# Experts' tiles in a new order, and the results of two groups of tokens fetched and normalised before the last scatters

## The chip, the cores and the metric

One core of a Trainium2 chip runs the whole kernel. The metric is the time of the device for one execution, in microseconds (us), as a median over runs. A TensorE (PE), a VectorE (DVE), a ScalarE (ACT), a GpSimd (POOL) and the queue of SyncE (SP) work beside each other and wait for each other by semaphores.

## The reference

The input x is 128 sequences of 64 tokens with 128 features, so 8192 tokens. Four layers are added to x one after the other, each behind a layer norm:

```
x = x + tanh(g_xattn[0]) * attention_16_heads(layernorm(x), ctx, ctx)        # heads of 8
x = x + tanh(g_ffn[0])   * experts(layernorm(x))                             # 8 experts, 2 per token, gelu, hidden 512
x = x + tanh(g_xattn[1]) * attention_1_head(layernorm(x), ctx, mask)         # tanh on the values
x = x + tanh(g_ffn[1])   * quantised_ffn(layernorm(x))                       # x and h rounded to 8 bits by their extremes
# experts: probs = softmax(x @ router.T); the two largest, divided by their sum, weigh
#          gelu(x @ w_fc[e] + b_fc[e]) @ w_proj[e] + b_proj[e]
```

## The kernel before, in words

Tokens stand 128 to a tile, four tiles make a group (QUAD, in the code also "super"), so there are 64 tiles in 16 groups; two groups are a chunk of 1024 tokens. The residual x stays in on-chip memory (`x_sb`) for the whole kernel. There are three programs (STAGES), with all engines meeting between them.

**First program, first attention and routing.** `layer0_and_experts` computes the first attention group by group. Beside it, VectorE picks two experts for every token, and POOL sends each token's normalised row twice by indirect DMA (L553) to `tokens_to`, a buffer in device memory with one region per expert. Rows come in the order of the tokens, so the first 1024 tokens lie in the first 1024 rows of their experts' regions at most.

**Experts.** The rows of an expert are cut into tiles of 512 rows (RT), some into half tiles of 256. There are ETILES = 40 places for them: EARLY = 13, whose numbers are known after five of eight chunks, and 27 late ones, nine times two full tiles and a half. Two tables say for each place at which row it begins and whose weights it takes. `early_tables` makes them in the first attention, in chained small operations of VectorE; `late_ends`, `tiles_and_halves`, `rows_and_jumps` and `half_tables` make the late ones piece by piece between the experts' tiles 4 to 7. In both, all tiles of expert 0 come first, then those of expert 1, and so on. SP loads a tile's rows (L350) and weights (L358, L368) in the order of the places; PE multiplies, ScalarE and VectorE take the sums, and POOL scatters the results by indirect DMA (L572), four instructions for a full tile, two for a half, to `results`, where each token has two rows. `returned` counts landed scatters in a ring of eight tiles (YRING).

**The seam.** When all scatters are back, SP loads `results` of groups 0, 1, 2 and 3 to 4 (`load_two`, L1838) and the rows of a mask (L430). At the same time VectorE, PE and ScalarE quantise the last layer's weights (L1754 to L1769, L846 to L854), and ScalarE sends them to device memory (`w_out`). VectorE adds the two result rows of group 0 (`first_sums`) and takes its statistics; ScalarE normalises it. VectorE adds group 1. POOL's last work are constants for the next program (`terms`). The mask load waits for `w_out`.

**Second attention.** In `layer1_attention` each engine has a program of steps s = 0 to 17, one per group, written out in order. POOL adds the results of groups 2 and up (`add_results`, L1948 and L1950) and normalises groups 3 and up (`normalise`, L1956 and L1959). VectorE takes statistics (`rows_of`, L2102 and L2105), reciprocals of the deviations by BATCHES of groups (`factors`, L2110), maxima of the scores (L2121), and the weighted sums of two steps earlier (L2130 to L2136). ScalarE takes square roots by batch (`roots`, L1980), normalises groups 1 and 2 (L2000), evicts products and takes exponentials (L2024). In POOL's stream the order is:

```
        for n in range(SUMS_IN_FRONT, 7):
            add_results(n)
        for n in (3, 4):
            normalise(n)
            add_results(n + 4)
        for n in range(5, SUPERS):
            if n + 4 < SUPERS:
                add_results(n + 4)
            normalise(n)
```

A normalising waits for the reciprocals of its whole batch (`rstd_ready`), and statistics for POOL's addition (`pool_added`). The third program, `layer1_ffn`, is not touched.

## Time and profile before

| what | us |
|---|---|
| three runs | 921.99, 925.02, 928.18 (median 925.02) |
| the profiled execution | 912.86 |
| its span, first to last instruction | 911.0 |
| VectorE busy | 715.8 |
| PE busy | 711.5 |
| POOL busy | 578.8 |
| ScalarE busy | 570.3 |
| first expert's product to last scatter | 374.4 to 690 |
| second attention | 702.2 to 791.8 |

The shares of busy time are means over stages with different limits. All times of rows are those of the profiled execution, counted from its first instruction, and its own time is 12 us under the median of the runs.

### The profile page before, as it was taken

To read this page: it belongs to the slowest core of one execution; us is meant where nothing else is said; L and a number is where in the kernel's file an instruction comes from. 1 tells how busy PE (TensorE), PEld (TensorE's weight loads), DVE (VectorE), ACT (ScalarE), POOL (GpSimd) and SP (SyncE) were. 2 spreads that over 40 slices of the span, in tenths; PEclk is the share of its full clock that TensorE was granted. 3 is DMA by queue.
4 is the path that set the end of the run, shared out by engine and by line. 5 is a ranking of instruction groups with operands and counts; after the bars stand their busy time and mean duration, and the time that the engine had idled before them with its cause. 6 is when DMAs were issued, how large, how long until landed. Compare 5 with 4: busy or idle time off the path is not lost. (4 is left out here: it accounts for less than half of the span.)

```text
span 911.0 us, 19681 instructions
## 1 busy us (share of the span) xinstructions
PE 711.5 (78%) x6547; PEld 556.5 (61%) x6550; DVE 715.8 (79%) x1835; ACT 570.3 (63%) x1176; POOL 578.8 (64%) x565
## 2 busy tenths in 40 slices
PE   5888799999999998689088899897972788556535
PEld 3666677777777776567066687776761566322224
DVE  4999999888888988477075677777763699889988
ACT  4556466767666664565165566766653888578745
POOL 4575487788887777646755545564555996088820
PEclk9999899999999989899588999999995899876569
DMA  8413632413232223657267778887835933000005
GB/s 244 122 37 127 102 106 86 140 61 130 89 107 84 83 98 115 232 162 216 64 192 226 243 223 276 247 253 217 251 124 175 350 107 107 24 1 0 1 23 163
DMA packets 95428, 127.69 MB, mean 140 GB/s; under 512 B 20528, under 2 KB 65152, under 8 KB 94304
## 3 DMA queue, kind: packets, MB, share of 16 engines
q1 hardware_dynamic: 85760, 108.00, 39.0%
q0 software_dynamic: 8672, 17.99, 5.7%
q8 instruction: 54, 0.88, 0.4%
q10 hardware_dynamic: 896, 0.43, 0.2%
q14 instruction: 46, 0.38, 0.1%
HBM read 82.76 MB, written 43.53 MB: 139 GB/s over the span
## 5 line engine op out<-in xcount | busy, mean ns | idle before, releaser
L572 POOL DMA_INDIRECT m_results<-a_probs,e_to x142 | 144.2, 1015 | 110.2 <-ACT a_probs L805 65.4
L783 ACT ACTIVATE room<-a_ps_s,e_bias 128x512 f32<-128x512 f32 (+1 forms) x160 | 102.2, 651 | 101.2 <-PE a_ps_s L1089 48.9
L581 POOL TENSOR_TENSOR a_probs<-a_probs,a_top 128x1024 f32<-128x1024 f32 x64 | 122.0, 1907 | 66.6 <-DVE a_top L1633 65.2
L553 POOL DMA_INDIRECT m_tokens_to<-r_rows,r_place x128 | 129.7, 1013 | 34.3 <-issue 32.0
L1662 DVE CAST e_hp<-room 128x512 fp32r<-128x512 f32 (+1 forms) x160 | 67.2, 420 | 88.4 <-remote 39.7
L700 ACT ACTIVATE a_probs_t<-a_ps_pt 128x512 f32<-128x512 f32 x128 | 70.2, 592 | 84.0 <-PE a_ps_pt L989 82.8
L1664 DVE TENSOR_TENSOR e_hp<-room,e_hp 128x512 fp32r<-128x512 f32 (+1 forms) x160 | 103.2, 645 | 5.6
L973 PEld LDWEIGHTS a_ps_o<-a_vals,a_probs_t 128*64 128x64 f32 x2048 | 71.2, 144 | 30.6 <-issue 29.8
L1594 DVE TENSOR_TENSOR a_probs<-a_ps_s,a_mask 128x1024 f32<-128x1024 f32 x64 | 78.0, 1219 | 15.0 <-PE a_ps_s L870 8.3
L973 PE MATMUL a_ps_o<-a_vals,a_probs_t 128*64 128x18 f32 x2048 | 79.1, 217 | 8.4 <-issue 6.6
L1633 DVE TENSOR_REDUCE a_top<-a_probs 128x16 f32<-128x1024 f32 x64 | 77.2, 1206 | 0.1
L989 PE MATMUL a_ps_pt<-ident,a_probs 128*128 128x128 f32 x512 | 74.3, 293 | 2.0 <-DVE n_values L1412 1.5
L2430 DVE TENSOR_REDUCE d_hpeak<-d_hid 128x1 f32<-128x2048 f32 (+1 forms) x36 | 70.7, 2044 | 3.6 <-ACT d_hid L2329 3.6
L989 PEld LDWEIGHTS a_ps_pt<-ident,a_probs 128*128 128x128 f32 x512 | 64.4, 152 | 3.5 <-DVE n_values L1412 2.7
L1099 PE MATMUL a_ps_pt<-e_hp,e_weights 128*128 128x512 f32 (+1 forms) x100 | 40.0, 400 | 31.9 <-issue 31.9
L1085 PE MATMUL a_ps_s<-e_xt,e_weights 128*128 128x512 f32 (+1 forms) x160 | 64.9, 405 | 0.0
L1089 PE MATMUL a_ps_s<-e_xt,e_weights 128*128 128x512 f32 (+1 forms) x160 | 60.8, 380 | 3.1 <-DVE e_xt L1671 3.1
L1086 PE MATMUL a_ps_s<-e_xt,e_weights 128*128 128x512 f32 (+1 forms) x160 | 60.6, 379 | 0.0
L2329 ACT ACTIVATE d_hid<-d_ps_h,d_b,d_outscale 128x512 f32<-128x512 f32 x64 | 46.2, 779 | 8.7 <-PE d_ps_h L2369 7.1
L634 ACT ACTIVATE room<-a_ps,a_own_bk,a_own 128x512 f32<-128x512 f32 x64 | 44.7, 787 | 2.5 <-PE a_ps L890 2.5
L1117 PE MATMUL a_ps_pt<-ident,room 128*128 128x128 f32 x142 | 24.7, 294 | 22.2 <-ACT room L797 16.5
L805 ACT ACTIVATE a_probs<-a_ps_pt,room 128x128 f32<-128x128 f32 x142 | 40.8, 373 | 1.8 <-PE a_ps_pt L1117 1.0
(396 smaller groups left out, 1908.3 us busy)
## 6 DMA issues: line engine op xcount, KB each, us to landing
e_weights<-m_weights_to SPq DMA_DIRECT2D x80, 512.0 KB
m_weights_to<-r_parts SPq DMA_DIRECT2D x8, 1024.0 KB
room<-m_tokens_to SPq DMA_DIRECT2D x31, 264.0 KB
c_two<-m_results SPq DMA_DIRECT2D x3, 1536.0 KB, 11.8
a_ctx_in<-in_ctx_dram SPq DMA_DIRECT2D x17, 256.0 KB, 3.0
m_keys_t<-n_keys SPq DMA_DIRECT2D x16, 256.0 KB
m_values<-n_values SPq DMA_DIRECT2D x16, 256.0 KB
out_dram<-x_all SPq DMA_DIRECT2D x15, 256.0 KB, 2.3
```

The source lines that it names most:

```text
L553: pool.indirect_dma_start(tokens_to, bass.IndirectOffsetOnAxis(ap=place[:, k, q:q + 1], axis=0), rows[:, c % RING, q % CT, k, :], None).th ...
L572: pool.indirect_dma_start(results, bass.IndirectOffsetOnAxis(ap=to[:, v, r:r + 1], axis=0), y[:, v, r], None).then_inc(returned[v], 16)
L581: pool.tensor_tensor(probs[:, j], probs[:, j], top[:, j].unsqueeze(2).broadcast_to([P, HEADS, SEQ]), ALU.subtract).then_inc(shifted, 1)
L700: act.activation(probs_t[:, j % 2, 4 * h:4 * h + 4, :], ps_pt[h][:], ACT.Exp).then_inc(pt_sb, 1)
L783: act.activation(h[:, c, at], ps_h[c][:, at], ACT.Gelu_apprx_tanh, bias=bias[:, n % ROWS, c:c + 1]).then_inc(h_sb, 1)
L973: mm = pe.matmul(ps_o[SEQ * b:SEQ * b + SEQ, cols], probs_t[:, (j + 1) % 2, gr, SEQ * b:SEQ * b + SEQ], vals[(t - 3) // QUAD % 2][:, (j + ...
L989: mm = pe.transpose(ps_pt[h][:, k, :], probs[:, (t + 2) % 4, 8 * h + 2 * k:8 * h + 2 * k + 2] .rearrange("p j k -> p (j k)"), ident[:])
L1594: dve.tensor_tensor(probs[:, j].rearrange("p (i k) q -> p i k q", i=BANDS), ps_s[:, :, j % 2], mask[:].unsqueeze(1).unsqueeze(1).broadcast ...
L1633: dve.tensor_reduce(top[:, j], probs[:, j], AX_X, ALU.max).then_inc(top_ready, 1)
L1662: dve.tensor_copy(hp[:, c, 0, at], h[:, c, at]).then_inc(h_hi, 1)
L1664: dve.tensor_tensor(hp[:, c, 1, at], h[:, c, at], hp[:, c, 0, at].bitcast(F32), ALU.subtract).then_inc(h_lo, 1)
L2430: dve.tensor_reduce(hpeak[:, e, column:column + 1], h, AX_X, op).then_inc(hpeak_ready, 1)
```

## The change

The tables put tiles in two classes: first at most two full tiles of every expert (with the odd halves of experts that have fewer), then all others. So each table operation works on 16 classes (CLASSES) instead of 8 experts, on one partition. Whatever belongs to the first 1024 tokens is then at the latest in place FIRST_CHUNK_END - 1 = 33 of 40.

Behind its last weight load SP waits for the scatters up to place 33, then loads the results of groups 0 and 1 into an own buffer (`early_two`, in `pad`). VectorE adds them between its steps on the last layer's weights, takes statistics of eight tiles, and ScalarE normalises both groups. POOL's constants are made after tile 13's scatters. The loads for groups 2 to 4 stay where they were.

In the second attention VectorE adds group 2 itself. Step 0 no longer waits for normalisings of groups 1 and 2: ScalarE takes the root and normalises group 2 after the exponentials of group 0, and the root of groups 3 and 4 at the end of its step 0. POOL adds three groups in front instead of five, and stays three groups ahead of its normalising instead of four.

```diff
+CLASSES = 2 * EXPERTS
+FIRST_TWO = 2 * QUAD
+FIRST_CHUNK_END = EARLY + 3 * (EXPERTS - 1)
...
+    early_two = pad[:].rearrange("p e r w -> p (e r w)")[:, 0:4 * ST].rearrange("p (s t k c) -> p s t k c", s=2, t=QUAD, k=2)
...
-    f_rows, f_mv = stats[:, 0:QUAD], mv[:, 0:QUAD]
-    f_std, f_rstd, f_nmr = (n[:, 0:QUAD] for n in (rstd2, rstd, nmr2))
+    f_rows, f_mv = stats[:, 0:FIRST_TWO], mv[:, 0:FIRST_TWO]
+    f_std, f_rstd, f_nmr = (n[:, 0:FIRST_TWO] for n in (rstd2, rstd, nmr2))
...
+        for n in range(FIRST_CHUNK_END - YRING, FIRST_CHUNK_END):
+            sp.wait_ge(returned[n % YRING], rows_returned(n))
+        for n in range(2):
+            load_two(sp, g, n, early_two[:, n:n + 1])
...
-        for n in range(EARLY_LOADS):
+        for n in range(2, EARLY_LOADS):
             load_two(sp, g, n, two[:, TWO_LOADS[n][0]:TWO_LOADS[n][1]])
...
         for n in range(1, ETILES):
             return_results(n)
-        pool.memset(magic[:, 0:1], MAGIC).then_inc(terms, 1)
-        pool.memset(magic[:, 1:2], -MAGIC).then_inc(terms, 1)
...
-        pool.wait_ge(terms, 12)
+            if n == EARLY:
+                pool.memset(magic[:, 0:1], MAGIC).then_inc(terms, 1)
+                pool.memset(magic[:, 1:2], -MAGIC).then_inc(terms, 1)
+                pool.memset(eps[:], LN_EPS).then_inc(terms, 1)
...
+                pool.wait_ge(terms, 12)
...
-        act.wait_ge(f_mv_ready, QUAD)
+        act.wait_ge(f_mv_ready, FIRST_TWO)
         act.activation(f_std[:], f_mv[:, :, 1], ACT.Sqrt, bias=power[:, 0, 0:1]).then_inc(f_std_ready, 1)
...
-        for k in range(QUAD):
-            act.activation(xn[:, 0, k], x_sb[:, k], ACT.Identity, scale=f_rstd[:, k:k + 1], bias=f_nmr[:, k:k + 1])\
+        for k in range(FIRST_TWO):
+            act.activation(xn[:, k // QUAD, k % QUAD], x_sb[:, k], ACT.Identity, scale=f_rstd[:, k:k + 1], bias=f_nmr[:, k:k + 1])\
                 .then_inc(f_xn_ready, 1)
...
-            then(dve.tensor_reduce(experts, passed, AX_X, ALU.add))
-            then(dve.tensor_reduce(rows_at, jumps, AX_X, ALU.add))
+        def beside_classes(x, n):
+            return x[:, 1:].unsqueeze(1).broadcast_to([1, n, CLASSES])
+
+        def early_look_up():
...
+            then(dve.tensor_tensor(early_jump[:], early_past[:], skip.unsqueeze(1).broadcast_to([1, EARLY, CLASSES]), ALU.mult))
+            then(dve.tensor_reduce(experts, early_past[:], AX_X, ALU.add))
+            then(dve.tensor_reduce(rows_at, early_jump[:], AX_X, ALU.add))
             then(dve.scalar_tensor_tensor(out=rows_at, in0=numbers, scalar=float(RT), in1=rows_at,
                                           op0=ALU.mult, op1=ALU.add))
-            then(dve.tensor_scalar(experts, experts, EXPERTS - 1.0, None, ALU.min))
+            then(dve.tensor_scalar(least, experts, float(EXPERTS), -float(EXPERTS), ALU.is_ge, ALU.mult))
+            then(dve.tensor_tensor(experts, experts, least, ALU.add))
...
+                then(dve.memset(one16, 1.0))
+                then(dve.memset(tile_end, 0.0))
+                then(dve.memset(odd_end, 0.0))
+                then(dve.memset(row_at, float(EXPERTS * REGION)))
+                then(dve.memset(odd_at, float(EXPERTS * REGION)))
+                then(dve.tensor_tensor(count, total[0:1, :, 0], base[0:1], ALU.subtract))
+                then(dve.tensor_scalar(ntile, count, 1.0 / RT, -0.5 + 0.5 / RT, ALU.mult, ALU.add))
+                then(dve.tensor_scalar(ntile, ntile, MAGIC, MAGIC, ALU.add, ALU.subtract))
+                then(dve.tensor_scalar(vt[:, 0:EXPERTS], ntile, 2.0, None, ALU.min))
+                then(dve.tensor_tensor(vt[:, EXPERTS:], ntile, vt[:, 0:EXPERTS], ALU.subtract))
+                then(dve.tensor_scalar(skip, vt, -float(RT), float(REGION), ALU.mult, ALU.add))
+                last = skip[:, EXPERTS - 1:EXPERTS]
+                then(dve.tensor_scalar(last, last, float(2 * RT - EXPERTS * REGION), None, ALU.add))
             if nth == 1:
-                tile_ends()
-                look_up(EARLY)
+                then(dve.tensor_tensor_scan(tile_end[:, 1:], one16, vt, 0.0, ALU.mult, ALU.add))
+                early_look_up()
...
+                then(dve.tensor_scalar(capped, tile_end, float(EARLY), None, ALU.min))
+                then(dve.tensor_tensor(used16, capped[:, 1:], capped[:, 0:CLASSES], ALU.subtract))
+                then(dve.tensor_tensor(used, used16[:, 0:EXPERTS], used16[:, EXPERTS:], ALU.add))
...
+                beside(dve.tensor_tensor(vt[:, EXPERTS:], ntile, vt[:, 0:EXPERTS], ALU.subtract))
+                beside(dve.scalar_tensor_tensor(out=row_at[:, EXPERTS:CLASSES], in0=vt[:, 0:EXPERTS], scalar=float(RT),
+                                                in1=row_at[:, 0:EXPERTS], op0=ALU.mult, op1=ALU.add))
+                beside(dve.scalar_tensor_tensor(out=oddv[:, 0:EXPERTS], in0=gone, scalar=2.0, in1=odd[:],
+                                                op0=ALU.is_lt, op1=ALU.mult))
+                for n in range(2):
+                    beside(dve.scalar_tensor_tensor(out=odd_at[:, EXPERTS * n:EXPERTS * n + EXPERTS], in0=gone,
+                                                    scalar=float(RT), in1=base[0:1], op0=ALU.mult, op1=ALU.add))
+            if turn == 3:
+                beside(dve.tensor_tensor_scan(tile_end[:, 1:], one16, vt, 0.0, ALU.mult, ALU.add))
+                beside(dve.tensor_tensor(oddv[:, EXPERTS:], odd[:], oddv[:, 0:EXPERTS], ALU.subtract))
+                beside(dve.tensor_tensor(odd_jump, odd_at[:, 1:], odd_at[:, 0:CLASSES], ALU.subtract))
+                beside(dve.tensor_tensor(skip, row_at[:, 1:], row_at[:, 0:CLASSES], ALU.subtract))
...
-            if t == 7 and turn < 2:
+            if t == 7 and turn < 3:
...
 
+        def first_sums(n):
+            four = slice(n * QUAD, n * QUAD + QUAD)
+            dve.wait_ge(two_in[n], 16)
+            dve.tensor_tensor(early_two[:, n, :, 0], early_two[:, n, :, 0], early_two[:, n, :, 1], ALU.add).then_inc(f_summed, 1)
+            dve.wait_ge(f_summed, n + 1)
+            dve.tensor_tensor(x_sb[:, four], x_sb[:, four], early_two[:, n, :, 0], ALU.add).then_inc(f_added, 1)
+
         dve.memset(w_magic[:, 0:1], MAGIC).then_inc(w_dve, 1)
         dve.memset(w_magic[:, 1:2], -MAGIC).then_inc(w_dve, 1)
         dve.wait_ge(w_in2, 32)
         for n in range(2):
             dve.tensor_reduce(w_peak[:, n:n + 1], w[:, n].rearrange("p a b -> p (a b)"), AX_X, ALU.max,
                               apply_absolute_value=True).then_inc(w_dve, 1)
+        first_sums(0)
         dve.wait_ge(w_pe, 1)
         dve.tensor_reduce(w_both, ps_h[2][0:2, 0:P], AX_X, ALU.max).then_inc(w_dve, 1)
         dve.wait_ge(w_pe, 2)
         dve.tensor_scalar(wscale[:], ps_h[3][:, 0:2], 1.0 / 127.0, 1e-8, ALU.mult, ALU.max).then_inc(w_dve, 1)
         dve.wait_ge(w_dve, 6)
         dve.reciprocal(w_inv[:], wscale[:]).then_inc(w_dve, 1)
+        first_sums(1)
         for n in range(2):
             dve.wait_ge(w_act, n + 1)
             dve.tensor_scalar(w[:, n], w[:, n], MAGIC - 127.0, MAGIC + 127.0, ALU.max, ALU.min).then_inc(w_dve, 1)
 
-        def first_sums(n):
-            four = slice(n * QUAD, n * QUAD + QUAD)
-            dve.wait_ge(two_in[n], 16)
-            dve.tensor_tensor(two[:, n, :, 0], two[:, n, :, 0], two[:, n, :, 1], ALU.add).then_inc(f_summed, 1)
-            dve.wait_ge(f_summed, n + 1)
-            dve.tensor_tensor(x_sb[:, four], x_sb[:, four], two[:, n, :, 0], ALU.add).then_inc(f_added, 1)
-
-        first_sums(0)
-        dve.wait_ge(f_added, 1)
...
-        for k in range(QUAD):
+        dve.wait_ge(f_added, 2)
+        for k in range(FIRST_TWO):
             dve.bn_stats(f_rows[:, k], x_sb[:, k]).then_inc(f_stats, 1)
-        for k in range(QUAD):
+        for k in range(FIRST_TWO):
...
-        first_sums(1)
...
-BATCHES = ((0, 1), (1, 2), (2, 3), (3, 5), (5, 8), (8, 12), (12, 16))
+BATCHES = ((0, 2), (2, 3), (3, 5), (5, 8), (8, 12), (12, 16))
...
-SUMS_IN_FRONT = 2
+SUMS_IN_FRONT = 3
...
+        for n in range(SUMS_IN_FRONT, 6):
             add_results(n)
         for n in (3, 4):
             normalise(n)
-            add_results(n + 4)
+            add_results(n + 3)
         for n in range(5, SUPERS):
-            if n + 4 < SUPERS:
-                add_results(n + 4)
+            if n + 3 < SUPERS:
+                add_results(n + 3)
             normalise(n)
 
...
         def roots(n):
             of = slice(BATCHES[n][0] * QUAD, BATCHES[n][1] * QUAD)
-            act.wait_ge(mv_ready, (BATCHES[n][1] - 1) * QUAD)
+            act.wait_ge(mv_ready, (BATCHES[n][1] - 2) * QUAD)
...
         evict_x(0)
-        roots(1)
-        normalise(1)
         act.wait_ge(ahead_in, 96)
         evict_q(0)
         evict_x(1)
-        roots(2)
-        normalise(2)
-        roots(3)
         for s in range(SUPERS + 1):
...
+            if s == 0:
+                roots(1)
+                normalise(2)
             if s + 2 < SUPERS:
                 evict_x(s + 2)
-            if s in (1, 5, 8):
-                roots({1: 4, 5: 5, 8: 6}[s])
+            if s in (0, 1, 5, 8):
+                roots({0: 2, 1: 3, 5: 4, 8: 5}[s])
...
+        dve.wait_ge(two_in[load_of[2]], 16)
+        dve.tensor_tensor(two(2)[:, :, 0], two(2)[:, :, 0], two(2)[:, :, 1], ALU.add).then_inc(dve_summed, 1)
+        dve.wait_ge(dve_summed, 1)
+        dve.tensor_tensor(x_sb[:, tiles(2)], x_sb[:, tiles(2)], two(2)[:, :, 0], ALU.add).then_inc(dve_summed, 1)
+        rows_of(2)
         dve.wait_ge(ahead_in, 96)
         dve.tensor_copy(more_terms[:], term_k[:]).then_inc(terms_copied, 1)
-        for n in range(1, NORMALISED_BY_ACT):
-            rows_of(n)
-            factors(n)
-            less_mean(n)
+        step(0)
+        factors(1)
+        less_mean(2)
         rows_of(3)
         rows_of(4)
-        step(0, 3)
+        step(1, 2)
         rows_of(5)
         rows_of(6)
-        for s in range(1, SUPERS + 2):
-            step(s, {2: 4, 6: 5, 9: 6}.get(s))
+        rows_of(7)
+        for s in range(2, SUPERS + 2):
+            step(s, {2: 3, 6: 4, 9: 5}.get(s))
```

## Rows read from the trace of the kernel before

**Rows 1.** Stages: start:end, us, busy (instructions) per engine, clock, DMA share, GB/s.

```profile
500.00:600.00 100.00, 90.19 (x489) 76.10 (x488) 71.95 (x158) 66.75 (x151) 56.29 (x55) 0.98 0.82 246
...
702.00:712.00 10.00, 7.23 (x21) 4.44 (x21) 6.66 (x25) 4.95 (x13) 9.43 (x8) 0.50 0.86 286
...
722.00:790.00 68.00, 55.63 (x367) 43.09 (x367) 64.25 (x250) 53.19 (x161) 42.59 (x39) 1.00 0.34 108
```

**Rows 2.** Timeline of the seam: start us, us, engine, line, what [idle before <-releaser].

```profile
683.26 0.28 DVE L1761 TENSOR_REDUCE a_bias_rest<-a_ps_s 2x1 f32<-2x128 f32 x1 [1.92 <-PE a_ps_s L1179]
...
688.99 0.96 POOL L572 DMA_INDIRECT m_results<-a_probs,e_to  x1 [0.30 <-issue]
...
691.12 0.36 ACTq L854 DMA_DIRECT2D c_weights_out<-a_probs_t  x1
...
695.46 0.69 DVE L1773 TENSOR_TENSOR room<-room 128x512 f32<-128x512 f32 x1 [8.17 <-DMA room<-m_results]
...
698.83 1.65 ACT L859 ACTIVATE room<-x_all,r_nmr,rstd 128x128 f32<-128x128 f32 x4 [0.44 <-DVE r_nmr L1787]
```

**Rows 3.** Timeline, SP's queue at the seam.

```profile
669.61 0.01 SPq L368 DMA_DIRECT2D e_weights<-m_weights_to  x1
...
691.31 2.29 SPq L1838 DMA_DIRECT2D room<-m_results  x4
...
693.71 1.97 SPq L430 DMA_DIRECT2D term_k<-c_mask_rows  x2
...
702.23 0.39 SPq L1838 DMA_DIRECT2D c_two<-m_results  x1
```

**Rows 4.** Timeline, first 22 us of the second attention.

```profile
704.13 2.05 PE L2046 MATMUL c_ps_q<-c_xn_t,wq 128*128 128x512 f32 x2 [0.78 <-ACT c_xn_t L1986]
...
708.82 0.63 PE L2057 MATMUL c_ps_s<-term_k,term_q 65*128 65x512 bf16 x1
...
709.24 1.91 PE L2061 MATMUL c_ps_s<-keys,c_q 128*128 128x128 f32 x8
...
713.65 0.67 ACT L1992 ACTIVATE c_q<-c_ps_q,bq 128x512 f32<-128x512 f32 x1
...
714.33 1.28 ACT L2024 ACT_TABLE_LOAD   x1
...
715.63 0.37 ACT L2024 ACTIVATE c_probs<-c_ps_s,c_ntop 128x128 f32<-128x128 f32 x1
...
717.18 0.66 PE L2076 MATMUL c_ps_pt<-ident,c_probs 128*128 128x128 f32 x4 [1.09 <-ACT c_probs L2024]
...
723.61 0.23 DVE L2110 RECIPROCAL rstd<-c_std 128x12 f32<-128x12 f32 x1 [1.88 <-ACT c_std L1980]
```

**Rows 5.** Timeline, POOL in the second attention.

```profile
715.16 1.05 POOL L1956 TENSOR_TENSOR room<-x_all,c_mv 128x512 f32<-128x512 f32 x1
...
742.78 1.04 POOL L1956 TENSOR_TENSOR room<-x_all,c_mv 128x512 f32<-128x512 f32 x1 [1.51 <-DVE rstd L2110]
...
755.65 1.27 POOL L1950 TENSOR_TENSOR x_all<-x_all,c_two 128x512 f32<-128x512 f32 x1
```

**Rows 6.** Timeline, ScalarE before the root of groups 8 to 11.

```profile
740.06 1.28 ACT L1980 ACT_TABLE_LOAD   x1
...
741.94 0.31 ACT L1980 ACTIVATE c_std<-c_mv,eps 128x16 f32<-128x16 f32 x1 [0.60 <-DVE c_mv L2105]
```

**Rows 7.** Timeline, VectorE's statistics of groups 12 and 15.

```profile
745.53 0.86 DVE L2102 BATCH_NORM_STATS2 c_rows_in<-x_all 128x6 f32<-128x128 f32 x4
...
756.96 0.87 DVE L2102 BATCH_NORM_STATS2 c_rows_in<-x_all 128x6 f32<-128x128 f32 x4 [0.71 <-POOL x_all L1950]
```

**Rows 8.** Groups by line, tables: what, count | busy us, mean ns | idle before.

```profile
L1436 DVE TENSOR_TENSOR r_past<-r_tnum,r_tile_end 128x104 f32<-128x104 f32 x1 | 0.3, 269 | 0.0
...
L1451 DVE TENSOR_TENSOR r_count<-r_total,r_base 128x8 f32<-128x8 f32 x1 | 0.2, 168 | 0.0
```

**Rows 9.** Waits from 425 to 462 us: total, times, longest.

```profile
PE a_ps_pt L1099 <- issue: 27.7, 1, 27.7
```

More of the change, by code:

```diff
@@ L1486, in late_ends @@
             if turn == 4:
-                beside(dve.tensor_scalar(ntile[0:1], halves[:], 0.5, -0.25, ALU.mult, ALU.add))
+                beside(dve.tensor_scalar(ntile, halves[:], 0.5, -0.25, ALU.mult, ALU.add))
         def tiles_and_halves(turn):
@@ new lines, in rows_and_jumps @@
+                beside(dve.tensor_scalar(over, half_slots[:, 1], float(EXPERTS), -float(EXPERTS), ALU.is_ge, ALU.mult))
+            if turn == 3:
+                beside(dve.tensor_scalar(trow[0:1], trow[0:1], row_at[:, 0:1], None, ALU.add))
+                beside(dve.tensor_scalar(texp[0:1], texp[0:1], EXPERTS - 1.0, None, ALU.min))
+                beside(dve.scalar_tensor_tensor(out=half_slots[:, 0], in0=half_slots[:, 0], scalar=odd_at[:, 0:1],
+                                                in1=idle_row[:], op0=ALU.add, op1=ALU.add))
+                beside(dve.tensor_tensor(half_slots[:, 1], half_slots[:, 1], over, ALU.add))
@@ L1538, in rows_and_jumps @@
                     dve.tensor_copy(slots, late_full[what].rearrange("p (g i) -> p g i", i=2)).then_inc(tables_ready, 1)
-                beside(dve.scalar_tensor_tensor(out=half_slots[:, 0], in0=half_slots[:, 0], scalar=first_odd[:, 0:1],
-                                                in1=idle_row[:], op0=ALU.add, op1=ALU.add))
+                second = late_half[0][:, 1:].rearrange("p (g i) -> p g i", i=2)[:, :, 1]
+                beside(dve.tensor_scalar(second, second, float(HALF_RT), None, ALU.add))
                 beside(dve.tensor_scalar(half_slots[:, 1], half_slots[:, 1], EXPERTS - 1.0, None, ALU.min))
-                second = late_half[0][:, 0:LATE_TRIPLES - 1].rearrange("p (g i) -> p g i", i=2)[:, :, 1]
-                beside(dve.tensor_scalar(second, second, float(HALF_RT), None, ALU.add))
-            if turn == 4:
-                for what in range(2):
-                    beside(dve.tensor_tensor(half_less[:, what], late_half[what], half_slots[:, what], ALU.subtract))
         def half_tables(turn):
@@ L1960, in normalise @@
                                ALU.mult).then_inc(xn_ready, 1)
-        for n in range(SUMS_IN_FRONT, 7):
+        for n in range(SUMS_IN_FRONT, 6):
             add_results(n)
```

169 lines of the change are left out of this document (80 added, 89 removed).

## The prediction

> **What bounds the kernel now.** I read the table of busy time by stage first, then the timeline of the seam between the experts and the second attention, then the waits of that attention engine by engine. The stage table [rows 1] shows the second attention (702 to 790 us) as VectorE's: from 722 on it is busy 64.25 of 68 us. In the ten us before 712 it is busy 6.66 while POOL is busy 9.43. So what the change is worth in this stage is the moment at which VectorE gets into its dense run, plus whatever makes it wait later. The page gives VectorE 715.8 us in all, an average that says nothing about the seam.
>
> **The seam.** The last scatter ends near 689.95 [rows 2]. SP sees it landed and issues four loads of results from 691.31 to 693.60, then the two mask loads until 695.68 [rows 3]. VectorE waits 8.17 us for the first load, sums at 695.46, takes statistics, and ScalarE normalises group 0 until 700.48 [rows 2]. The next program starts at 702.23 [rows 3], 1.75 us after the last engine ended. I call that moment T = 0.
>
> **Part 1, results of two groups fetched early.** Removed from the tail: the wait for their landing, the sums, statistics and the normalising. SP now issues the two loads behind the last weight load (669.61 [rows 3]), and tile 33's scatter is long out: 20 scatters are behind it, each takes at least 0.96 + 0.30 us of issue, and the last starts at 688.99 [rows 2], so it was issued before 663.8. They are landed by 676 at the 4.1 us that the first load needs now (691.31 to 695.46 [rows 2, 3]). VectorE's two pairs of sums take 1.4 us each: the first fits in the idle 1.92 us before 683.26 [rows 2], the second in the time in which ScalarE loads a table (1.28) and scales the weights before the first clip. What is left: eight statistics (0.86 for four [rows 7]) and eight aggregates behind the last clip, done near 689.7; ScalarE's square root waits for its own weight store (issued 691.12 to 691.48), so 691.8; reciprocal and factor 692.25; eight normalisings at 1.65 us for four, 3.3 us: 695.55. SP still waits for that weight store to land before the masks, 695.68. Both end together. Plus 1.75 us: the attention starts at 697.45, **4.8 us earlier**. Bounds: 5.5 us if the mask issue shrinks, 3 us if ScalarE's eight take longer. POOL's 3.25 us of constants move from behind the last scatter to tile 13; nothing waited for them at the end, and POOL is busy 56.29 of 100 us there [rows 1], so zero; uncovered they would cost 3.25.
>
> **Part 2, the new start of the attention (T of its own).** Here the order of the work changes, and I walk the chain.
> - The queries of group 0 end at T 3.95 as now (704.13 + 2.05 [rows 4]). Eviction 0.67 [rows 4], so 4.65. The transposes of group 1 are in front of the scores and end at 5.05. Scores of group 0 take 2.33 (mask 708.82, end 711.15 [rows 4]): 7.4. Queries of group 1 (1.7): 9.1. Eviction of 0.67: 9.8.
> - The exponentials of group 0 take 2.85 from the start of their table load to PE's transposes [rows 4]: 12.65. Today three square roots and two normalisings stand ahead of them; now those of groups 2 to 4 stand behind.
> - So ScalarE switches back: table load 1.28, root 0.30: 14.2. Reciprocal and factor 0.35. Normalising group 2, 1.65 as for group 0 [rows 2]: 16.3. Transposes and eviction 1.3: 17.6. Root of groups 3 and 4: 17.9, VectorE's reciprocal: **18.2**. (VectorE's statistics of 3 and 4 run from 14.6 to 17.1, just covered.)
> - POOL has only three groups to add first (five fill 12.9 us today, so T 7.7), then waits for that reciprocal to normalise group 3. Now it starts that at 715.16, T 12.9 [rows 5]. Queued behind it on POOL are the additions of groups 6 and 7. A pair of one normalising and one addition is 4.70 us (742.78 to 756.92 are three pairs [rows 5]); two pairs: T 27.6.
> - VectorE's statistics of group 7 wait for this: done T 28.8, and the root that ScalarE holds for it comes at 29.2. VectorE's first weighted sums start at T 29.75; today at T 21.5 (right after the reciprocal at 723.61 [rows 4]). 8.25 later in T, less 4.8 of the seam: **+3.45 us**.
>
> The work behind is the same and dense (64.25 of 68), so this is carried on.
>
> **A rule on table loads.** ScalarE's table load takes 1.28 us and stands in front of the wait of its activation (load at 740.06, root at 741.94 after 0.60 us of waiting [rows 6]). So the load ahead of the root at T 28.8 is hidden, and the two others on the chain cost 1.28 each. The Trainium skill ("ScalarE: Activation LUTs", What ACT_TABLE_LOAD costs) puts a switch at 1.28 us and a drain of 1.38 on top. By that rule, as an estimate, the chain is 2.8 us longer and the sum 11.6. The load at 714.33 with the next activation 1.30 later [rows 4] shows no such drain here.
>
> **Part 3, POOL's lead is one group shorter.** Before, POOL has added up to group 12 when it waits for the factors of groups 8 to 11; after, up to group 11. From that point R (742.78 now [rows 5]) group 12 ends at R + 4.70 instead of before R, and group 15 at R + 18.8 instead of R + 14.1. VectorE wants group 12 at 745.53, R + 2.75 [rows 7]: it waits 2.0. It would want group 15 at 756.25 (it waits 0.71 even now, to 756.96 [rows 7]); with the 2.0 it is R + 15.5, and waits 3.3 more. Its start moves by 18.8 - 14.1 = **+4.65 us** in all. ScalarE's root of the last batch is held until group 15 has its statistics, and the exponentials of group 9 stand behind that root, so I take no slack behind it. Bounds: 2.0, if the pipeline had 2.7 us to spare there, and 4.7.
>
> **Part 4, tables.** Six more chained operations in the early tables at about 0.17 each and four at twice the elements (0.27 for 104 [rows 8]), some 1.5 us on VectorE in the first attention; about 2 us more between experts' tiles 4 to 7. VectorE is busy 71.95 of 100 us among the experts [rows 1], so most of the latter fall into its gaps. I take 0.7; bounds 0 and 3.5. Tiles and halves are the same in number; only their order changes, zero. The table chain is due before tile 13, tens of us later.
>
> **Sum:** 3.45 + 4.65 + 0.7 = +8.8 us. In the profiled execution's own time 912.86 gives 921.7. The median of the three runs is 925.02, 12 us above that execution; the same step gives **934**. About 9.25 us (1%) is what a measurement can tell from no change; this sum is just under it.
>
> **Rivals.**
> - *The seam pays for the new start.* If PE or ScalarE pass the start 3.5 us faster than walked (the start is at half clock, 0.50 [rows 1], and the walk takes that clock for group 0), only part 3 and the tables are left: +5.35, 930.4. For it: I kept the half clock for every product up to T 9 and it may rise sooner. Against: every link is in order on its engine.
> - *The seam's gain is kept (the other side).* The place is POOL's first normalising. If the reciprocal of groups 3 and 4 is there by T 12.9, VectorE enters its dense run at T 21.5, 4.8 us earlier in all; and if then its waits of part 3 fall in gaps, the result is -4.8 + 0.7: 921. For it: nothing in PE's or VectorE's work forbids it. Against: the root stands behind four exponentials, two table loads and a normalising on ScalarE. It decides from 5.3 us of slack on that chain, which I do not see.
> - *The hole among the experts moves.* PE shows 27.7 us without work before a product at 459.5 [rows 9], at 430 to 460, with engines handing on at 5 to 7 us each. What makes it is not in the trace, and VectorE's table operations of tiles 4 and 5, which change, lie in it. Gone it gives 906, doubled 962; PE's own instructions there do not change, which speaks against either.
> - *The early results are not early.* If the loads wait for their tiles' scatters or land late, the seam is as now and parts 2 and 3 stay: +13.6, 939.
>
> **Chances.** Forecast 0.56 (slower by over 1% 0.32, within 0.24: the open prices, half clock behind T 9 and the tables' 3.5, lie above the sum). Seam pays 0.16, within. Gain kept 0.12 (within 0.10, faster by over 1% 0.02). Hole 0.10, half each side. Not early or other 0.06 (faster 0.02, within 0.01, slower 0.03). Faster 0.09, same 0.51, slower 0.40. The range reaches from the kept gain, 922, to the forecast with the upper bounds of start and tables, 942.
>
> **What would show it.** The attention's first instruction about 8.5 us after the last scatter's start instead of 13.2 (part 1). POOL idle some 10 us before its first subtraction of a mean, at T 18, and ScalarE standing before the root of the third batch until T 28.8 (part 2). VectorE waiting for POOL's sums at groups 12 and 15, 2.0 and 3.3 us (part 3). If POOL does not idle before its first subtraction, the forecast is wrong.

## The result

The changed kernel takes 929.31 us (median of 9 runs, 924.3 to 934.37), the kernel before 921.27 (9 runs, 914.37 to 928.18): a ratio of **1.0123, 95% interval 1.0091 to 1.0155**, slower by 1.2%. The medians alone are 8.04 us (0.9%) apart, just under that interval, so the loss is some 8 to 11 us. The profiled executions are 924.3 and 912.86 us, +11.4. The prediction was 934 (922 to 942), its sum +8.8 us. It gave "slower by over 1%" a chance of 0.40 and "within 1%" 0.51; the interval holds both. All ratios below compare the faster of two states that executions fall into, and only order back has its profile from the slower one (911.3 us).

**Stages.** First the stage table of the kernel after (columns as in [rows 1]).

```profile
550.00:680.00 130.00, 116.79 (x643) 98.31 (x642) 94.58 (x211) 86.23 (x199) 72.58 (x70) 0.99 0.81 245
...
698.50:708.50 10.00, 7.16 (x22) 4.34 (x23) 4.45 (x12) 3.04 (x7) 6.95 (x6) 0.59 1.00 320
708.50:718.50 10.00, 4.77 (x19) 3.44 (x20) 4.30 (x29) 7.42 (x18) 1.80 (x3) 0.75 1.08 358
718.50:728.50 10.00, 5.16 (x28) 3.81 (x26) 2.97 (x19) 5.88 (x14) 9.69 (x9) 0.84 0.61 205
728.50:802.00 73.50, 60.23 (x365) 49.18 (x365) 64.53 (x250) 51.02 (x159) 40.87 (x37) 0.89 0.24 76
```

VectorE has the same dense work at the end (64.53 us; 64.25 in [rows 1]), but it now takes 73.5 us instead of 68, and 30 us pass before it in which VectorE is busy 11.7.

**The seam.** Timeline of the kernel after, from the last scatter to the next program.

```profile
683.13 0.69 DVE L1792 TENSOR_TENSOR r_pad<-r_pad 128x512 f32<-128x512 f32 x1
...
685.67 0.72 DVE L1792 TENSOR_TENSOR r_pad<-r_pad 128x512 f32<-128x512 f32 x1
...
690.95 0.36 ACTq L872 DMA_DIRECT2D c_weights_out<-a_probs_t  x1
...
692.04 0.96 POOL L589 DMA_INDIRECT m_results<-a_probs,e_to  x1 [0.30 <-issue]
692.13 3.19 ACT L877 ACTIVATE room<-x_all,r_nmr,rstd 128x128 f32<-128x128 f32 x8 [0.47 <-issue]
694.36 0.93 SPq L1873 DMA_DIRECT2D room<-m_results  x2
695.40 0.68 SPq L444 DMA_DIRECT2D term_k<-c_mask_rows  x2
698.58 0.39 SPq L1873 DMA_DIRECT2D c_two<-m_results  x1
```

The sums of both groups stand among the weights' work, without the 8.17 us of waiting of [rows 2]. From the last scatter's start to the next program it is 6.54 us, where [rows 2, 3] have 13.24.

**The second attention.** POOL's timeline in the kernel after (T 0 is 698.58).

```profile
701.32 1.26 POOL L1983 TENSOR_TENSOR room<-room 128x512 f32<-128x512 f32 x1 [8.32 <-DMA room<-m_results]
...
707.85 1.26 POOL L1985 TENSOR_TENSOR x_all<-x_all,c_two 128x512 f32<-128x512 f32 x1
717.24 1.04 POOL L1991 TENSOR_TENSOR room<-x_all,c_mv 128x512 f32<-128x512 f32 x1 [8.12 <-DVE rstd L2144]
...
748.36 1.04 POOL L1991 TENSOR_TENSOR room<-x_all,c_mv 128x512 f32<-128x512 f32 x1 [4.92 <-DVE rstd L2144]
```

Its first subtraction of a mean is at T 18.7, after 8.1 us without work; [rows 5] have it at T 12.9. VectorE's timeline in the kernel after, its long waits:

```profile
712.87 0.18 DVE L2144 RECIPROCAL rstd<-c_std 128x4 f32<-128x4 f32 x1 [5.31 <-ACT c_std L2015]
...
722.00 0.87 DVE L2136 BATCH_NORM_STATS2 c_rows_in<-x_all 128x6 f32<-128x128 f32 x4 [3.83 <-POOL x_all L1985]
...
726.68 0.87 DVE L2136 BATCH_NORM_STATS2 c_rows_in<-x_all 128x6 f32<-128x128 f32 x4 [3.53 <-POOL x_all L1985]
...
753.12 0.87 DVE L2136 BATCH_NORM_STATS2 c_rows_in<-x_all 128x6 f32<-128x128 f32 x4 [1.93 <-POOL x_all L1985]
767.20 0.87 DVE L2136 BATCH_NORM_STATS2 c_rows_in<-x_all 128x6 f32<-128x128 f32 x4 [3.52 <-POOL x_all L1985]
...
774.41 0.69 DVE L2155 TENSOR_REDUCE c_ntop<-c_ps_s 128x4 f32<-128x512 f32 x1 [1.55 <-PE c_ps_s L2093]
```

The first is the square root of group 2 behind the exponentials, then come the statistics of groups 6 and 7; the fourth and fifth are groups 12 and 15, which answer to [rows 7]. The last one is new and was not in the prediction. Nor was a wait of TensorE, whose queries of group 0 stand behind the load of the mask (timeline of the kernel after):

```profile
701.65 2.07 PE L2078 MATMUL c_ps_q<-c_xn_t,wq 128*128 128x512 f32 x2 [1.95 <-DMA term_k<-c_mask_rows]
```

They start at T 3.1; in [rows 4] it is T 1.9.

### The profile page after: what moved, and what is told of

It reads as the page before. It is cut to its first block and busy times, and to the rows that moved or that the text cites. A ratio compares the mean times of both kernels' runs of the same rounds, so it can differ in the third digit from the quotient of the medians.

```text
span 922.5 us, 19699 instructions
## 1 busy us (share of the span) xinstructions
PE 725.5 (79%) x6547; PEld 571.5 (62%) x6550; DVE 718.2 (78%) x1851; ACT 571.4 (62%) x1177; POOL 580.9 (63%) x564
## 5 line engine op out<-in xcount | busy, mean ns | idle before, releaser
L589 POOL DMA_INDIRECT m_results<-a_probs,e_to x142 | 147.2, 1037 | 99.6 <-ACT a_probs L823 48.2
L598 POOL TENSOR_TENSOR a_probs<-a_probs,a_top 128x1024 f32<-128x1024 f32 x64 | 121.9, 1905 | 67.8 <-DVE a_top L1668 66.2
L991 PEld LDWEIGHTS a_ps_o<-a_vals,a_probs_t 128*64 128x64 f32 x2048 | 74.3, 150 | 29.0 <-issue 28.2
L1629 DVE TENSOR_TENSOR a_probs<-a_ps_s,a_mask 128x1024 f32<-128x1024 f32 x64 | 78.1, 1220 | 13.9 <-PE a_ps_s L888 9.2
L991 PE MATMUL a_ps_o<-a_vals,a_probs_t 128*64 128x18 f32 x2048 | 82.3, 221 | 6.9 <-issue 5.5
L1007 PE MATMUL a_ps_pt<-ident,a_probs 128*128 128x128 f32 x512 | 76.5, 299 | 1.3 <-DVE n_values L1430 1.0
L1007 PEld LDWEIGHTS a_ps_pt<-ident,a_probs 128*128 128x128 f32 x512 | 66.7, 156 | 2.9 <-DVE n_values L1430 2.1
L1016 PE MATMUL a_ps_o<-ident,a_heads 128*128 128x128 f32 x64 | 21.0, 328 | 28.6 <-DVE x_all L1612 27.5
L1601 DVE RECIPROCAL a_rsum<-a_ps_o 128x16 f32<-128x16 f32 x64 | 16.2, 252 | 33.7 <-PE a_ps_o L998 17.3
## 6 DMA issues: line engine op xcount, KB each, us to landing
c_two<-m_results SPq DMA_DIRECT2D x3, 1536.0 KB, 11.7
```

The costliest lines, as they stand in the source:

```text
L589: pool.indirect_dma_start(results, bass.IndirectOffsetOnAxis(ap=to[:, v, r:r + 1], axis=0), y[:, v, r], None).then_inc(returned[v], 16)
L598: pool.tensor_tensor(probs[:, j], probs[:, j], top[:, j].unsqueeze(2).broadcast_to([P, HEADS, SEQ]), ALU.subtract).then_inc(shifted, 1)
L991: mm = pe.matmul(ps_o[SEQ * b:SEQ * b + SEQ, cols], probs_t[:, (j + 1) % 2, gr, SEQ * b:SEQ * b + SEQ], vals[(t - 3) // QUAD % 2][:, (j + ...
L1007: mm = pe.transpose(ps_pt[h][:, k, :], probs[:, (t + 2) % 4, 8 * h + 2 * k:8 * h + 2 * k + 2] .rearrange("p j k -> p (j k)"), ident[:])
L1629: dve.tensor_tensor(probs[:, j].rearrange("p (i k) q -> p i k q", i=BANDS), ps_s[:, :, j % 2], mask[:].unsqueeze(1).unsqueeze(1).broadcast ...
```

## The experiments

The first program (first attention and experts) is the same code in after, five sums first, lead of four, both on POOL and the two with the order back, yet in these six executions its last scatter starts between 684.84 and 693.95 us. So each kernel is also read by stage from its trace: the seam (last scatter's start to the next program's first load), the first weighted sum in T, and from there to the last group of them. All in us, of one profiled execution each; a star marks the executions of 830 to 845 us, told of below.

| kernel | seam | first sum | from there to the last | attention | ratio to before (95%) |
|---|---|---|---|---|---|
| before | 13.24 | 21.5 | 65.0 | 86.5 | 1 |
| after | 6.54 | 29.9 | 72.2 | 102.1 | 1.0123 (1.0091 to 1.0155) |
| control* | 6.53 | 29.3 | 71.9 | 101.2 | 1.0105 (1.0091 to 1.0119) |
| late fetch | 17.54 | 27.8 | 71.3 | 99.1 | 1.0276 (1.0218 to 1.0333) |
| five sums first | 7.83 | 25.2 | 70.5 | 95.7 | 1.0168 (1.0109 to 1.0226) |
| the same again* | 6.54 | 26.0 | 70.4 | 96.5 | 1.0075 (1.0046 to 1.0104) |
| lead of four | 7.80 | 28.3 | 66.3 | 94.6 | 1.0113 (1.0040 to 1.0186) |
| both on POOL | 11.61 | 26.2 | 65.0 | 91.2 | 1.0072 (1.0028 to 1.0117) |
| group 2 first* | 6.52 | 23.1 | 66.4 | 89.5 | 0.9965 (0.9941 to 0.9988) |
| order back | 11.57 | 18.6 | 65.5 | 84.1 | 1.0007 (0.9966 to 1.0047) |
| masks early* | 6.54 | 19.7 | 66.2 | 85.9 | 0.9939 (0.9921 to 0.9958) |
| order back, lead of three | 6.52 | 22.1 | 70.1 | 92.3 | 0.9979 (0.9922 to 1.0037) |
| tables alone | 13.18 | 22.0 | 65.0 | 87.0 | 1.0055 (1.0017 to 1.0093) |
| the same again* | 13.00 | 22.0 | 65.6 | 87.6 | 1.0028 (1.0005 to 1.0051) |

The column ends at the start of the last timeline row of weighted sums, which holds four of them; the expectations end at the start of the last single one, 0.7 to 0.9 us more.

**Five sums first.**
```
-        for n in range(SUMS_IN_FRONT, 6):
+        for n in range(SUMS_IN_FRONT, 8):
             add_results(n)
         for n in (3, 4):
             normalise(n)
-            add_results(n + 3)
```


> One part of the new start undone: POOL adds five groups (3 to 7) before its first normalising instead of three, and nothing between the two first normalisings; its lead stays one group shorter from group 5 on. Theory (VectorE's late start is POOL's: the additions of groups 6 and 7 stand behind the first normalising while POOL idles 8.1 us in front of it): the two additions fill that idle time, VectorE's waits of 3.83 and 3.53 us before the statistics of groups 6 and 7 go, the first weighted sums come at T 23 to 25 instead of 29.9, and the kernel is 5.5 us shorter than the changed one (4 to 7), 1.006 of the kernel before. The waits at groups 12 and 15 (1.9 and 3.5) stay. Rival (the start is bound by TensorE's half clock and ScalarE's table loads): the waits change their releaser from POOL to PE or ACT and the gain is 0 to 2 us.

Measured: the waits of 3.83 and 3.53 us are gone and POOL's idle time before its first subtraction falls from 8.12 to 2.85 us, but the first sum comes at T 25.2, 4.7 us earlier, not 5 to 7. VectorE meets another limit: its timeline in this kernel shows it waiting for ScalarE.

```profile
715.20 0.18 DVE L2143 RECIPROCAL rstd<-c_std 128x4 f32<-128x4 f32 x1 [5.58 <-ACT c_std L2014]
...
724.76 0.18 DVE L2149 RECIPROCAL c_gain<-c_rsum 128x4 f32<-128x4 f32 x1 [2.19 <-ACT c_probs L2052]
...
726.87 0.23 DVE L2143 RECIPROCAL rstd<-c_std 128x12 f32<-128x12 f32 x1 [1.33 <-ACT c_std L2014]
```

So both readings hold in part: the stage gains, and of the 7.4 us of waits that went, 3.5 come back as waits for ScalarE. Its time did not show the gain (1.0168). So it was measured again:

> The five additions first once more, beside the control's 1.0105. The trace of the first run showed the attention 6.4 us shorter (96.5 against 102.9), its time did not (1.0168 against 1.0123). Theory (the time is the first program's noise, the stage is real): 1.002 to 1.005 where executions agree, the stage 96 to 97 us. Rival (what POOL's front gives is taken elsewhere): 1.009 or more.

The stage came out the same (96.5). The ratio, 1.0075, lies 0.0030 below the control's, 2.5 us, but on another chip and with intervals that overlap (up to 1.0104, from 1.0091), so the time alone does not show a gain; by the stages it is 4.8 us. It lies above the 1.002 to 1.005 I expected and under the rival's 1.009. Taking 4.8 us from the control would give 1.005; what keeps the ratio 2 us above that is not shown.

**Lead of four.**
```
         for n in range(5, SUPERS):
-            if n + 3 < SUPERS:
-                add_results(n + 3)
+            if n == 8:
+                add_results(n + 3)
+            if n + 3 + (n >= 8) < SUPERS:
+                add_results(n + 3 + (n >= 8))
             normalise(n)
```


> The other part undone: start as changed (three groups added first), but POOL makes one addition more where it waits for VectorE before the normalising of group 8 (4.9 us idle), so that from there it leads by four groups as in the kernel before. Theory: VectorE's waits of 1.93 us at group 12 and 3.52 us at group 15 go, and the stretch at half clock behind the second with them; 5.5 us shorter than the changed kernel (4 to 7). The first weighted sums stay at T 29.9. Rival (these waits are slack behind another limit): the waits go, others of the same size appear behind them, 0 to 1 us.

Measured: first sum at T 28.3, and from there 66.3 instead of 72.2, 5.9 us; both waits are gone. VectorE's timeline here, groups 12 and 15:

```profile
747.99 0.86 DVE L2138 BATCH_NORM_STATS2 c_rows_in<-x_all 128x6 f32<-128x128 f32 x4
...
760.07 0.85 DVE L2138 BATCH_NORM_STATS2 c_rows_in<-x_all 128x6 f32<-128x128 f32 x4
```

The rival (other waits of the same size) is out as a whole, though one wait that the kernel after lacks is there, VectorE's for TensorE's scores:

```profile
750.73 0.69 DVE L2157 TENSOR_REDUCE c_ntop<-c_ps_s 128x4 f32<-128x512 f32 x1 [1.53 <-PE c_ps_s L2095]
```

The ratio moved by 0.001 only, within its interval of 0.007; the stage carries this verdict, not the time.

**Both on POOL.**
```
-        for n in range(SUMS_IN_FRONT, 6):
+        for n in range(SUMS_IN_FRONT, 8):
             add_results(n)
-        for n in (3, 4):
-            normalise(n)
-            add_results(n + 3)
+        normalise(3)
+        add_results(8)
+        normalise(4)
         for n in range(5, SUPERS):
-            if n + 3 < SUPERS:
-                add_results(n + 3)
+            if n + 4 < SUPERS:
+                add_results(n + 4)
             normalise(n)
```


> Both of POOL's parts undone, nothing else: five additions (3 to 7) first, then normalising 3, addition 8, normalising 4, then addition n+4 before normalising n. Theory: the two prices add, 10 to 12 us shorter than the changed kernel, 1.000 of the kernel before (0.997 to 1.003). Rival (one limit behind both): no more than the larger of the two alone.

Measured: 10.9 us less attention than after, 6.4 from five sums and 7.5 from the lead taken singly, 13.9 in sum; so the two overlap by some 3 (the seams differ, and with them the start). The ratio 1.0072 includes a seam of 11.61 us: here the weights' store is issued at 695.87 instead of before the last scatter, and the mask follows at 701.76. The program before the seam is the same, so this is not the edit. Attention and seam together are 5.9 us shorter than after, the ratios say some 5, not the 10 to 12 I expected.

**Group 2 first**, on top of both POOL parts.
```
         evict_x(1)
+        roots(1)
+        normalise(2)
         for s in range(SUPERS + 1):
...
-            if s == 0:
-                roots(1)
-                normalise(2)
...
-        step(0)
         factors(1)
         less_mean(2)
+        step(0)
```


> The kernel with both of POOL's parts undone, and in it only the square root and the normalising of group 2 before the exponentials of group 0; statistics and root of groups 3 and 4 stay behind. It splits the 7.2 us that lie between both POOL parts undone (92.0 from the attention's start to its last weighted sum) and the whole old order (84.8). Theory (two table loads and a root on ScalarE are what stands in the way): one load less on the chain and group 2 early, 89 to 91 us. Rival (it is the statistics of groups 3 and 4 behind the first maximum): 91.5 to 92.5.

Measured: 90.2 by the expectation's count, first sum 3.1 us earlier than with POOL alone. VectorE's first maximum, in step 0, moves behind group 2's factors with it. ScalarE's timeline shows the root before the exponentials, with no table load of its own:

```profile
627.59 0.29 ACT L2015 ACTIVATE c_std<-c_mv,eps 128x4 f32<-128x4 f32 x1
629.30 1.65 ACT L2034 ACTIVATE room<-x_all,c_nmr,rstd 128x128 f32<-128x128 f32 x4 [1.42 <-DVE c_nmr L2173]
...
634.84 1.28 ACT L2015 ACT_TABLE_LOAD   x1
636.13 0.30 ACT L2015 ACTIVATE c_std<-c_mv,eps 128x8 f32<-128x8 f32 x1
```

Between 91.2 and 84.1 lie 7.1 us, both with the long seam of 11.6. This kernel has the short seam, with which the attention loses up to 1.8 us (order back against masks early, below). So moving group 2 brings 1.7 us as it stands (89.5), and up to 3.5 with equal seams; against masks early, which has the short seam too, 3.6 remain. They lie in what the next kernel has besides: statistics and root of groups 3 and 4 ahead of the exponentials, without this load, and four additions instead of five ahead of POOL's first normalising. I did not split these. At 0.9965 (0.9941 to 0.9988) this kernel is 2.9 us faster than before.

**Order back**: ScalarE, VectorE and POOL in the order of the kernel before, only without group 1 (in short):
```
+        roots(1); normalise(2); roots(2)        # ScalarE, ahead of the exponentials
+        rows_of(3); rows_of(4); step(0, 2); rows_of(5); rows_of(6)     # VectorE
+        for n in range(SUMS_IN_FRONT, 7): add_results(n)               # POOL, then +4
```


> The seam as changed (two groups' results early), the second attention in the order of the kernel before: roots and normalising of group 2 before the exponentials of group 0, statistics of groups 3 and 4 before the first maximum, POOL with its old lead. Theory: the seam's 6.7 us are kept and the start costs no more than before: 15 us shorter than the changed kernel (12 to 17), 0.993 to 0.998 of the kernel before if the 3.0 us of the tables stay, the first weighted sums at T 21 or earlier. Rival (a start that comes earlier meets loads that are not there): VectorE waits for the results' loads and the gain over the kernel before is gone, 1.000 to 1.005.

Measured: the attention is 84.1, 2.4 us shorter than before; the first sum at T 18.6. The ratio, 1.0007, does not show it; the profiled execution has the long seam of 11.57, the others' seams are not known. Seam and attention together are 13 us shorter than after. What the rival feared shows in masks early below, with the short seam: POOL waits until T 2.7 for its first load, and the attention is 1.8 us longer than here.

**Order back, lead of three** (in short):
```
+        # POOL as changed: three additions first, then +3; the rest as in order back
```


> As the kernel with the early seam and the old order of ScalarE and VectorE, but POOL as changed: three additions first and a lead of three. Theory: POOL's lead is a price of its own, 4.65 us by the forecast (2.0 to 5.5), whatever the start: this kernel is that much longer than the same with POOL's old order, and 8 to 12 us shorter than the changed kernel. Rival: with the first normalising early, POOL has time, and the lead costs nothing.

Measured: the first sum 3.5 us later (22.1 against 18.6), from there 70.1 against 65.5, **4.6 us**, at the two waits that the prediction named:

```profile
737.25 0.87 DVE L2136 BATCH_NORM_STATS2 c_rows_in<-x_all 128x6 f32<-128x128 f32 x4 [1.94 <-POOL x_all L1985]
...
751.31 0.87 DVE L2136 BATCH_NORM_STATS2 c_rows_in<-x_all 128x6 f32<-128x128 f32 x4 [3.52 <-POOL x_all L1985]
```

This kernel has the short seam and order back the long one. Against masks early, which has the short one too, the first sum is 2.4 us later and the rest 3.9 longer; TensorE also waits here for the mask, as in the kernel after. So the lead costs 3.9 to 4.6 us behind the first sum with the old order as well. The ratios of this pair were measured on two chips and don't tell them apart.

**Late fetch**: the seam undone.
```
-        for n in range(2):                      # behind the first chunk's scatters
-            load_two(sp, g, n, early_two[:, n:n + 1])
+        for n in range(2):                      # behind the last scatter
+            load_two(sp, g, n, early_two[:, n:n + 1])
```


> The seam undone, nothing else: the results of groups 0 and 1 are fetched behind the last scatter and summed behind the last clip, all eight tiles before the next program. Theory (forecast's part 1): the seam is the 13.2 us of before plus the second group's sums (1.4), statistics (0.9) and normalising (1.65), 8 to 10 us longer than the changed kernel, 1.022 of the kernel before. Rival (the early loads cost the experts as much as they spare at the seam): 0 to 4 us longer.

Measured: the seam is 17.54 us, 11.0 more; timeline of its wait:

```profile
679.36 0.93 SPq L1871 DMA_DIRECT2D r_pad<-m_results  x2
...
683.34 0.69 DVE L1790 TENSOR_TENSOR r_pad<-r_pad 128x512 f32<-128x512 f32 x1 [8.70 <-DMA r_pad<-m_results]
```

The attention behind it is 3.1 us shorter, so 7.9 in the two stages. Its own loads have then landed: POOL starts at T 0 (after: T 2.7), but idles 7.8 us all the same before its first subtraction; on the chain is the mask, for which TensorE does not wait here, and its first queries start at T 1.9 instead of 3.1. The ratio is 0.0153 above after's, 14 us, with some 6 us of interval and from two sessions. The rival is out: the early loads pay at the seam.

**Tables alone**: the kernel before with the new tables.
```
+            then(dve.tensor_scalar(vt[:, 0:EXPERTS], ntile, 2.0, None, ALU.min))
+            then(dve.tensor_tensor(vt[:, EXPERTS:], ntile, vt[:, 0:EXPERTS], ALU.subtract))
...
```


> The kernel before with the new tables alone: the order of the experts' tiles, the constants that it needs and VectorE's chained table operations; fetch, seam and second attention as before. Forecast: +0.7 us (0 to 3.5). Theory from the trace of the changed kernel, where the experts start 3.0 us later (377.4 against 374.4) and the last scatter 3.05 later: +3.0 us. Rival: those 3.0 are the clock of that execution (0.874 against 0.889), and the tables cost 0 to 1 us.

> The new tables alone once more, because the first measurement (1.0055 of the kernel before, 1.0017 to 1.0093) was made where identical first programs differ by 9 us. Forecast's term: +0.7 us (0 to 3.5), ratio 1.000 to 1.002. Theory from that first measurement: +5 us, ratio above 1.003. The sum of the measured stages of the control (seam -6.6, attention +14.7, whole +8.8) leaves 0.7 for the tables.

Measured: +5.0 us (1.5 to 8.4), then +2.3 (0.4 to 4.3) where executions agree better. Seam and attention are those of before in both. I take 2.3: above the 0.7 of the sum, inside its bounds. The 3.0 us at the experts' start are no evidence: in the first execution the last scatter even starts 6.5 us earlier than before's.

**Control**, the kernel after once more, and **masks early**, the masks' move (in short) on top of order back.
```
+        sp.wait_ge(terms, 10)
+        # the two mask loads, ahead of the waits for the last scatters
         for v in range(YRING):
             sp.wait_ge(returned[v], ...)
...
         sp.wait_ge(w_out, 16)
```


> The changed kernel itself, unchanged, as the reference for the two beside it and for the stages: six executions of the same first program so far ended between 684.8 and 694.0 us, so one profile does not give its length. Theory (the second attention carries the loss): from its start to its last weighted sum 101 to 104 us again (87.3 before), the ratio to the kernel before 1.010 to 1.018. Rival (the traces' stages vary as much as the first program does): below 98 us, ratio under 1.008.

> The kernel with the early seam and the old order, and in it the two loads of the mask put ahead of the last scatter's wait on SP's queue, the wait for the weights' store left alone at its end. Theory: the seam is then bound by that store's landing and ScalarE's eight normalisings, 0.7 to 1.5 us shorter, the attention 84.8 us as without it (83.5 to 86.5), 0.990 to 0.998 of the kernel before. Rival (the tables and the early loads cost the first program what the seam gives): 1.000 to 1.005.

Control: 846.02 against 837.71 us, ratio 1.0105, which is **+8.8 us (7.6 to 10.0)**. Masks early: 0.9939, **5.1 us faster than before** (3.5 to 6.6), on the same chip. The move of the masks itself gave nothing at the seam, 6.54 with it and 6.53 without. Behind it TensorE's first queries start at T 1.9 instead of 3.1, since they no longer wait for the mask. What beats the kernel before is the early seam with the old order; how much of the 5.1 us is the mask's I did not split. SP's last issue there is the pair of loads at 617.79 to 618.73, and the next program starts at 622.02; what fills those 3.3 us is not in the trace.

## Why the prediction was right

**Part 1, seam, -4.8.** Measured -6.7 (13.24 to 6.54, 6.5 in six of the ten profiled executions with the early fetch, 7.8 in two and 11.6 in two). SP's issues end 4.0 us after the last scatter's start, 2.65 earlier than walked: the two loads that left the queue (0.93 instead of 2.29 us) and a shorter mask issue (0.68 instead of 1.97, [rows 3]). The next program starts 2.5 us after SP instead of 1.75, which leaves 1.9. My bound of 5.5 was too narrow. In the six executions with 6.5 ScalarE's weight store is issued before the last scatter starts; I had it 2.1 us behind, as before. Where it comes 1.7 us behind the seam is 7.8, and 3.2 us behind 11.6; these four executions are of one session. ScalarE's eight normalisings took 3.19 us as summed (3.3).

**Part 2, start, +8.25 in T.** Measured +8.4 (29.94 against 21.52) and +7.8 in the control. The links: root of group 2 ends at T 14.3 (14.2 walked), POOL's first subtraction starts at T 18.66 (18.2), first sum T 29.94 (29.75). Three links were wrong. POOL ends its three additions at T 10.5, not 7.7, because it waits until T 2.7 for a load; harmless, it still idles 8.1 us. TensorE's queries of group 0 wait for the mask and end at T 5.1, not 3.95. And the clock rises sooner than I took it: between T 7.9 and T 9.9 TensorE has a granted 0.96, and the queries of group 1 take 1.02 us, not 1.7. These two nearly cancel, so that the exponentials end at T 12.6 as walked (12.65); that is luck. The experiments show the composition: the old order on ScalarE and VectorE alone takes the first sum from T 29.9 to 22.1, POOL's five additions alone to 25.2 or 26.0, everything back to 18.6 (19.7 with the short seam). Each hides part of the other.

**Part 3, lead, +4.65.** The two waits measured 1.93 and 3.52 us (2.0 and 3.3 forecast). 0.71 of it was there before, so 4.74 more, as forecast. But from the first sum to the last it is 72.2 us against 65.0 before, +7.2. A term was left out: VectorE now also waits for TensorE's scores, 0.39, 1.55 and 0.33 us, none of which is in the kernel before. The longest follows the wait for group 15: TensorE has nothing for 6.29 us, and comes back at a granted 0.58. Windows of the kernel after, then of lead of four, around that point:

```profile
766.00:769.00 3.00, 0.00 (x0) 0.00 (x0) 1.80 (x11) 0.62 (x2) 1.16 (x1) 0.85 0.00 0
769.00:776.00 7.00, 6.68 (x28) 5.79 (x28) 4.81 (x17) 4.80 (x13) 4.16 (x4) 0.58 0.24 75
776.00:779.00 3.00, 3.00 (x26) 2.96 (x27) 2.62 (x9) 2.57 (x10) 1.26 (x2) 1.00 0.27 70
```

```profile
759.00:762.00 3.00, 1.01 (x4) 0.18 (x2) 3.00 (x21) 1.77 (x3) 2.44 (x3) 1.00 0.34 125
762.00:769.00 7.00, 6.13 (x44) 5.15 (x45) 6.36 (x23) 6.44 (x21) 4.38 (x5) 1.00 0.24 76
```

The eight products of a group take 2.08 us at a granted 0.58 and 1.16 us in the other kernel at 1.00, and VectorE's maximum then waits 1.55 us for its scores. In the six executions with a lead of three, each with 6.2 to 6.3 us without a product there, this wait is 0.64 to 1.55 us, so its price varies. The 5.9 us between after and lead of four are mostly the two waits whole, 5.45, since lead of four has no 0.71 before group 15; its own wait of 1.53 us for scores nearly makes up for the 1.55.

**Part 4, tables, +0.7.** Measured +2.3 (0.4 to 4.3): undersized.

**The sum.** +8.8 forecast; the control, where five executions lie within 2 us, gives +8.8 (7.6 to 10.0). Its stages give -6.7 + 14.7 = +8.0, which leaves 0.8 for the tables; with the 2.3 of the tables alone it would be 10.3, just outside, and in the other starred kernels the same count leaves 0.8 to 3.0, so the tables' size stays in that range. That the total fits so well is partly luck: the seam was 1.9 too small a gain, the attention 1.8 too short, the tables too cheap. In the first pair the ratio says +11.3 (8.4 to 14.3). The range's upper end, 942, stands 8 us above the sum, more than the bounds of the seam (1.8) and the tables (2.8) give; the rest, half clock behind T 9, had no number.

**The rivals.** "The seam pays for the new start" fell: the clock did rise sooner, for 0.7 us in the queries of group 1, but the wait for the mask took that and the first sum was not earlier than walked. "The seam's gain is kept" needed POOL's normalising by T 12.9; it came at 18.7. With the order back it comes at T 11.2, with masks early at T 13.1, and the latter kernel is faster than before. "The hole moves": it stayed, 26.7 us (27.7 in [rows 9]). It is there, at 25.4 to 28.1 us, in all nine executions of over 900 us, with the new tables and without, and in none of the five of 830 to 845, the same code as after among them; so it is not the tables'. "Early results are not early": they were.

**The rule on table loads.** The trace speaks against the Trainium skill's 1.38 us of drain ("ScalarE: Activation LUTs", What ACT_TABLE_LOAD costs) here too: in the kernel after the exponentials end at about 711.2, the load starts at 711.25 and takes 1.28, and the root runs at 712.54. By its estimate the sum would have been 11.6; the control's interval ends at 10.0, the first pair's, up to 14.3, would allow it, so it is the trace that decides.

## What to carry to other kernels

Taking a wait out of a seam is worth what the next stage's critical engine gets of it: find that engine's first dense work, walk the in-order queues to it, and count what stands ahead of the one instruction that releases it. When work is moved ahead of a program boundary, leave the order behind it alone at first: here the early fetch with the old order gained 5 us, and the reordering that came with it cost 14 (with the small move of the masks in it). An adder that runs k groups ahead must be costed at the points where a batch closes: here the shorter lead showed at groups 12 and 15, and then once more where TensorE came back from its pause at a granted 0.58.

## What the runs showed of the hardware

- The kernel before took 905.66 to 921.27 us (medians) in three sessions and 834.33 and 837.71 in two others, on other chips; the changed kernel 929.31 and, as the control, 846.02. The hole in the experts is absent in all five profiles from those two sessions: in the control TensorE is busy all of 400 to 440 us, where the kernel after has 17.59 of 45 (425 to 470), and from first to last scatter of results it is 216.8 us instead of 271.7. Windows of the control, and of the kernel after:

```profile
400.00:440.00 40.00, 40.00 (x203) 33.10 (x202) 38.65 (x122) 30.75 (x64) 29.23 (x30) 1.00 0.85 272
```

```profile
425.00:470.00 45.00, 17.59 (x82) 14.05 (x81) 16.54 (x56) 11.37 (x23) 29.83 (x31) 0.71 0.43 126
```

  The hole is some 27 of the 79 us by which the last scatter comes earlier; the rest is spread. What makes it was not found. Kernels run in both kinds of session give the same attention to within 1 us, and the same seam to within 1.3.
- The next program's start follows the last scatter's start by 6.52 to 6.54 us in six executions of five different kernels, whether SP ends with the masks or without them. In all six the weights' store is issued before the last scatter; in the four of one session where it comes 1.7 or 3.2 us after it, it is 7.8 and 11.6 us.
